# Cross-attention and routed experts: attention on pairs of head groups in five chunks of 128 keys, with the neighbouring block's raw-row transposes and router logits moved

## What is computed

```
x = x + xattn(layernorm(x), ctx)       # q, k, v; softmax(q k^T * scale) v; relu(out @ W1 + b1) @ W2 + b2
logits = layernorm(x) @ Wg.T ; top1 = argmax(logits)
x = x + expert[top1](layernorm(layernorm(x)))   # gelu((xhat * s_e + b_e) @ w1 + bb1) @ w2 + bb2
```

## Time and profile before

| | before |
|---|---|
| median of 3 runs | 1548.81 us (1548.56 to 1552.27) |
| the profiled execution | 1549.81 us, of which 1548.0 us are its span |
| PE busy | 1503.9 us (97%) |
| DVE busy | 1005.6 us (65%) |
| ACT busy | 711.5 us (46%) |
| chain that ended last | PE 78%, DVE 14% |

### The profile page before, as it was taken

How to read it: one execution, slowest core, us unless ns; L and a number is a source line. 1 busy time by engine, 2 the same in 40 slices (tenths; PEclk the granted TensorE clock), 3 DMA queues, 4 the chain that set the end, 5 groups by cost and what they waited for, 6 DMA issues and landing times.

```text
span 1548.0 us, 24311 instructions
## 1 busy us (share of the span) xinstructions
PE 1503.9 (97%) x7988; PEld 1257.0 (81%) x7988; DVE 1005.6 (65%) x2489; ACT 711.5 (46%) x2015; POOL 428.8 (28%) x312
## 2 busy tenths in 40 slices
PE   7689999999999999999999999999999999999998
PEld 4578888888888787878788888888887878778986
DVE  5735656575857576666757585757574756559666
ACT  3534535354536363545445353535363635424554
POOL 2512212222222222212122112222222222117776
PEclk9799999999999999999999999999999999999999
DMA  9310110213020202131211201030202011458883
GB/s 231 113 55 28 31 53 7 76 26 108 13 89 28 89 28 75 36 97 42 75 42 40 78 15 61 16 110 1 82 1 83 1 55 55 171 172 282 243 238 120
DMA packets 76951, 122.71 MB, mean 79 GB/s; under 512 B 27990, under 2 KB 36455, under 8 KB 75806
## 3 DMA queue, kind: packets, MB, share of 16 engines
q1 hardware_dynamic: 66030, 87.47, 19.6%
q0 software_dynamic: 10800, 33.70, 5.7%
HBM read 76.24 MB, written 46.72 MB: 79 GB/s over the span
## 4 chain that ended last, share of the span: by engine, by line
PE 78%; DVE 14%; ACT 4%; issue 2%; DMA 1%; POOL 1%; POOLq 0%; DVEq 0%; SPq 0%; ACTq 0%
PE bank L1034 23%; PE bank L1056 20%; PE bank L896 11%; PE bank L920 5%; PE bank L1014 5%; DVE actH L1003 4%; PE bank L1457 4%; PE bank L1501 3%; ACT actH L997 2%; PE bank L1125 2%; PE bank L1440 2%; PE bank L864 2%; DVE E L941 1%; DVE mx L929 1%; DVE sm L968 1%
## 5 line engine op out<-in xcount | busy, mean ns | idle before, releaser
L1056 PE MATMUL bank<-w,actH 128*128 128x512 f32 x1536 | 371.1, 392 | 0.0
L1034 PE MATMUL bank<-actA,w 128*128 128x512 f32 x1536 | 366.8, 394 | 0.0
L1034 PEld LDWEIGHTS bank<-actA,w 128*128 128x128 f32 x1536 | 286.0, 188 | 62.3
L1056 PEld LDWEIGHTS bank<-w,actH 128*128 128x128 f32 x1536 | 283.1, 188 | 54.9
L979 POOL TENSOR_TENSOR E<-E,rc 128x1232 f32<-128x1232 f32 x64 | 145.0, 2266 | 464.6 <-DVE rc L974 464.6
L1041 ACT ACTIVATE actH<-bank,b 128x512 fp32r<-128x512 f32 x128 | 88.2, 689 | 228.8 <-PE bank L1034 228.8
L1046 DVE TENSOR_TENSOR actH<-bank,actH 128x512 fp32r<-128x512 f32 x128 | 87.8, 686 | 159.6 <-ACT bank L1042 159.6
L896 PE MATMUL bank<-actA,wq 128*128 128x512 f32 x768 | 182.0, 390 | 0.0
L952 ACT ACTIVATE E<-bank,mx 128x77 f32<-128x77 f32 x512 | 157.8, 364 | 42.1 <-DVE mx L929 42.1
L896 PEld LDWEIGHTS bank<-actA,wq 128*128 128x128 f32 x768 | 144.1, 188 | 30.4 <-issue 0.5
L1199 POOL DMA_INDIRECT region<-rows,pos x64 | 62.3, 974 | 373.2 <-DVE pos L1193 334.0
(11 more groups left out here) (166 smaller groups left out, 1970.2 us busy)
## 6 DMA issues: line engine op xcount, KB each, us to landing
rowB<-region SPq DMA_DIRECT2D x71, 258.0 KB, 3.8
xn<-in_x SPq DMA_DIRECT2D x64, 256.0 KB, 2.8
rows<-in_x SPq DMA_DIRECT2D x64, 256.0 KB, 3.2
e_raw<-in_E SPq DMA_DIRECT2D x16, 256.0 KB, 2.8
region<-padrow SPq DMA_DIRECT2D x9, 258.0 KB, 3.9
w_raw<-in_W SPq DMA_DIRECT2D x1, 2048.0 KB, 11.8
w_raw<-in_W SPq DMA_DIRECT2D x2, 1024.0 KB, 8.7
e_parts<-e_high SPq DMA_DIRECT2D x8, 256.0 KB, 2.0
```

Of the source, the lines that this page charges most:

```text
L1034: mm = pe.matmul(p[:], w, a, start=k == 0 and j == 0, stop=k == KD - 1 and j == 2)
L1056: mm = pe.matmul(p[:], a, w, start=m == 0 and j == 0, stop=m == MF - 1 and j == 2)
```

## The change

The groups are taken in pairs: 616 keys of a pair are cut in five chunks, four of 128 and one of 104. Per pair one chunk (number 2, called C) holds keys of both groups, so its product goes to a bank of its own; chunks 0 and 1 (A) make the first group and 3 and 4 (B) the second. ACT copies the bank of C to a new tile `csb` (COPY), and two DVE additions (ADD) put its 32 rows for each group onto the banks of A and B. OUT takes the parts out as before. So a block has 10 PT steps in place of 12, and 30 AV matmuls in place of 36, and new are 2 copies and 4 additions on 32 partitions.

Of the four TT of the block before, two stay in the tail, with their take-out (TTOUT) at its end; two go behind H steps 0 and 1. H 0 and 1 are issued together, k by k. X2STAT starts after the tail. L moves from after H 0 to after H 2, LT to after H 3, RK to after H 5 (H 4 in the last block). E1_SUM moves from after H 1 to after H 2. The values are loaded in 24 transfers in place of 12. Banks are no longer given out in turn but as the bank that is left first by the order of the list.

```
-CH = [103, 103, 102]
+NP = KD // 2
+PH = 2 * HG
+CH = [128, 128, 128, 128, 104]
+CA, CC, CB = (0, 1), (2,), (3, 4)
...
         def attention_tail(b):
             for c in range(NC):
                 step("PT", b, 0, c)
             step("SUM", b, KD - 1)
+            for c in CA:
+                step("PT", b, 1, c)
+            step("AV", b, 0, "C")
+            step("COPY", b, 0)
+            step("AV", b, 0, "A")
+            step("AV", b, 0, "B")
             if b:
-                step("X2STAT", b - 1)
-            for g in range(KD):
-                if g + 1 < KD:
-                    for c in range(NC):
-                        step("PT", b, g + 1, c)
-                if b and g == KD - 2:
-                    for s in range(SUB):
-                        step("TT", b - 1, s)
-                step("AV", b, g)
+                step("TT", b - 1, 0)
+                step("TT", b - 1, 1)
+            step("AV", b, 1, "A")
+            step("ADD", b, 0, "A")
+            step("ADD", b, 0, "B")
+            step("OUT", b, 0, "A")
+            for c in CC + CB:
+                step("PT", b, 1, c)
+            step("AV", b, 1, "C")
+            step("OUT", b, 0, "B")
+            step("COPY", b, 1)
+            step("AV", b, 1, "B")
+            step("ADD", b, 1, "A")
+            step("ADD", b, 1, "B")
+            step("OUT", b, 1, "A")
+            step("OUT", b, 1, "B")
+            if b:
+                step("TTOUT", b - 1, 0)
+                step("TTOUT", b - 1, 1)
...
+            if b:
+                step("X2STAT", b - 1)
             for m in range(MF):
                 step("H", b, m)
-                if prep is not None and m == 1:
+                if prep is not None and m == 2:
                     step("E1_SUM", prep)
+                if b and m == 2:
+                    step("L", b - 1)
...
+                step("HLO", b, m)
+                if b and m == 1:
+                    for s in (2, 3):
+                        step("TT", b - 1, s)
+                        step("TTOUT", b - 1, s)
...
+        def dve_add(dve, b, pr, i):
+            p, r = of("AV", b, pr, i), slice(P - HD, P) if i == "A" else slice(0, HD)
+            if i == "A":
+                dve.wait_ge(S["act_c"], NP * b + pr + 1)
+            dve.wait_ge(S["pe_av"], av_count(b, pr, i))
+            dve.tensor_tensor(p[r, :], p[r, :], csb[r, :], ALU.add).then_inc(S["dve_c"], 1)
```

More of the change, by code:

```diff
@@ L360, in xattn_moe_kernel @@
                     step("E1_ACC", prep)
-                if prep is not None and m == 1:
+                if prep is not None and m == 2:
                     step("E1_CENTER", prep)
                     step("E1_STORE", prep)
-                if b and m == 2:
-                    step("LT", b - 1)
-                    step("HLO", b, m)
                 if b and m == 3:
                     step("DRAIN")
+                    step("OH", b - 1)
+                if b and m == (4 if last else 5):
                     for s in range(SUB):
@@ L372, in xattn_moe_kernel @@
                         step("XLOAD", b + 1)
-                if last and m == MF - KD:
+                if last and m == 5:
                     step("COUNT", 0)
                     step("TABLE1")
-                if m == 3 and not last:
+                    step("DRIP", 8)
+                if m == (3 if prep is None else 4) and not last:
                     step("XSTAT", b + 1)
@@ L476, in xattn_moe_kernel @@
         }
-        bank_of, before, users = {}, {}, [None] * 8
-        n = 0
-        for kind, *i in sched:
+        LEAVES = {"COPY": lambda b, p: ("AV", b, p, "C"), "OUT": lambda b, p, i: ("AV", b, p, i),
+                  "TTOUT": lambda b, s: ("TT", b, s), "HLO": lambda b, m: ("H", b, m), "Y": lambda b, s: ("YA", b, s),
+                  "E1_CENTER": lambda e: ("E1_SUM", e)}
+        left = {}
+        for place, (kind, *i) in enumerate(sched):
+            left[(kind, *i)] = place
+            if kind in LEAVES:
+                left[LEAVES[kind](*i)] = place
+        bank_of, before, users, busy = {}, {}, [None] * 8, list(range(-8, 0))
+        for place, (kind, *i) in enumerate(sched):
             if kind in freed:
                 key = (kind, *i)
[L483 to L486, removed]
+                n = busy.index(min(busy))
+                assert busy[n] < place
+                bank_of[key] = n
+                before[key] = users[n]
+                users[n] = freed[kind](*i)
+                busy[n] = left[key]
         def own_bank(eng, *key):
@@ new lines, in av_count, with pe_av @@
+        def av_count(b, pr, i):
+            return len(AV_ORDER) * b + AV_ORDER.index((pr, i)) + 1
+        def pe_av(pe, b, pr, i):
+            p = own_bank(pe, "AV", b, pr, i)
+            if (pr, i) == AV_ORDER[0]:
+                pe.wait_ge(ld_v, 16 * VLOADS * (b // BPB + 1))
+            mine = {"A": CA, "B": CB, "C": CC}[i]
+            for c in mine:
+                j = NC * pr + c
+                pe.wait_ge(S["dve_pt"], NC * NP * b + j + 1)
+                for t, (v, w) in enumerate(split3([vbd[0:CH[c], h, pr, c, :] for h in range(2)],
@@ L1013, in pe_av @@
                                                   [actH[0:CH[c], h, j % SLOTS, :] for h in range(2)])):
-                    mm = pe.matmul(p[:], v, w, start=c == 0 and i == 0, stop=c == NC - 1 and i == 2)
+                    mm = pe.matmul(p[:], v, w, start=c == mine[0] and t == 0, stop=c == mine[-1] and t == 2)
             mm.then_inc(S["pe_av"], 1)
-        def act_av(act, b, g):
-            act.wait_ge(S["pe_av"], KD * b + g + 1)
-            act.activation(actA[:, 0, g, :], of("AV", b, g)[:], ACT.Identity).then_inc(S["act_o"], 1)
@@ L1024, in dve_av @@
                               ).then_inc(S["dve_o"], 1)
         def pe_h(pe, b, m):
-            p = own_bank(pe, "H", b, m)
+            if m == 1:
+                return
+            mine = (0, 1) if m == 0 else (m,)
+            for m in mine:
+                own_bank(pe, "H", b, m)
             if b == 0:
```

155 lines of the change are left out of this document (89 added, 66 removed).

## The result

| | before | after |
|---|---|---|
| median of 4 runs | 1549.14 us | 1570.54 us (1569.91 to 1572.32) |
| ratio, 95% interval | | 1.0136 (1.0118 to 1.0153) |
| span of the profiled execution | 1548.0 us | 1568.2 us |
| PE busy | 1503.9 us (97%) | 1480.0 us (94%) |

A forecast was written before the change was run, and what follows sets the result against it. PE, busy 97% of the span, was taken to bound the kernel. Tail - 24, block 0 - 2 and waits for L + 42 made + 16 us on 1549.81, 1565.8, predicted as 1565; range 1547 to 1582 us.

The forecast's parts named there:

- The tail: First PT to first H: 13.6 us with waits of 0.5 and 0.7; 1.6 won per block, 24 in 15 blocks.
- Block 0: After its first low part, nine AV matmuls in place of 18: 2 us won, bounds 0.5 and 4.
- ADD: DVE additions in the tail: 0.61 us each, bounds 0.15 and twice 0.61, costing nothing.
- When L starts: In the up-projection L waits for DVE's last TT take-outs: 3.61 us in each of 8 blocks, 1.88 in 7; sum 42.1.
- e + 1.31: DVE starts taking out H 0's low part 1.31 us after e, the modelled end of H 0's last matmul.
- The clock: PE's clock behind the new waits for L: expected to stay up, granted clock 0.9 or more, nothing counted.
- my case: Main forecast for the whole kernel: 1565 us, itself 1553 to 1577, chance 0.55.
- a rival: PE's clock falls in the new waits in all eight blocks, 2 us each: 1581 us; chance 0.15.
- The sum: Whole kernel: - 24 - 2 + 42 = + 16 us against the profiled 1549.81.
- Transfers: 24 value transfers delay the row load some 8 us in blocks 3, 7, 11; nothing counted; rival 1571, chance 0.07.
- Banks: Banks given out differently: each former user taken out before PE comes to it, so nothing counted.

The follow-up runs named there:

- spread_only: Kernel before with only the spreading (two TT and X2STAT out of the tail; L, LT, RK, E1_SUM later), without pairs or interleaving; 1560.1 us.
- unmerged: Changed kernel with H 0 and H 1 issued one after the other; 1549.3 us.
- l_late2: Changed kernel with L behind H 3, LT and the one-hot behind H 4, and XSTAT behind H 4 in every block; 1538.1 us.
- filler: Changed kernel with 18 needless PE transposes ahead of the wait for L in the eight blocks with preparation; 1560.2 us.
- l2_split: l_late2 with the 24 value transfers cut in two, twelve behind the tail and twelve behind the next block's XLOAD; 1529.9 us.
- tt_in_tail: Changed kernel with all four TT in the tail and their take-outs at its end; 1566.2 us.

## Why the prediction was right, and where it was off

1565 was forecast and 1570.5 measured, inside the range; the direction and its reason held: L came late by the take-outs moved behind H 0 and H 1, and the loss was larger than the tail's gain. That it came so close is in part luck. The waits were 10 us shorter than forecast (32 against 42), and the clock, counted at nothing, cost 12. By its own steps:

- **The tail.** 13.6 us forecast, 13.66 measured in 15 blocks. The two waits in it were 0.33 and 0.63, not 0.53 and 0.7; the matmuls between them made up for it. What I booked wholly on the pairs is theirs only by half: spread_only, which has the old tail without two TT, needs 14.5 us for it. Taking eight transposes (0.79 us) and X2STAT out of the old tail saved 1.5 us, because waits went with them.
- **Block 0.** 2 us forecast; block 1's tail starts 2.2 us earlier (153.54 against 155.76). One profile of each can't say more than that: in the other runs with the same block 0 it starts anywhere from 151.6 to 153.4.
- **ADD.** 0.61 us and hidden. It takes 0.70, the same for 32 partitions as a take-out for 128, and in the change PE waits for none. It is hidden by the interleaving: in unmerged H 0 does wait, 0.4 us, for the take-outs behind the ADDs.
- **When L starts.** DVE took H 0 out at 337.76, which by my working is e + 1.31, so L could start 6.67 us later, at 344.43; it started at 344.18. The order of DVE and its prices were right to 0.25 us. The waits are shown as 0.49 and 2.26, 2.75 against my 3.61, and as 1.45 against 1.88. Part of that is the way of counting: the trace counts from the modelled end of the matmul before, I from where the next could have started. l_late2 shows what the wait of 1.45 truly cost, 1.57 us (82.1 to 80.53).
- **The clock.** This is the term that was mis-sized: my case had it at nothing, and a rival had it with a chance of 0.15 and 2 us. It fell in all eight blocks, at 1.4 to 1.7 us each, 12 us. Rival and case came true together: period + 2.8 to + 3.2 with preparation, where I had + 2.0, and + 0.1 where I had + 0.3. I had called the wait shorter than all that I saw followed by a low clock, and looked only at its longer piece.
- **The sum.** By the measured terms: tails 15 x 1.56 = - 23.4, block 0 - 2.2, waits 8 x 2.75 + 7 x 1.45 = + 32.2, clock + 12; that gives + 19, and the spans differ by 20.2. The agreement is closer than it should be. Where the last tail starts (1330.60 against 1307.53, 23.1 us later) the terms give 19, so 0.3 us a block is not in them, the way of counting above among it; and what follows that start is 2.9 us shorter (237.6 against 240.5 us). No run shows that to be the change's doing: in the filler the program there is the same, and that part took 240.7.
- **Transfers.** Rightly counted at nothing here. They take 0.80 us each, and the last rows' load starts 37.5 us behind the tail's start in place of 30.9 (355.29 and 350.58); yet blocks 3 and 7 were no longer than their neighbours. My reading, which no run tests by itself, is that with L's wait and the low clock ahead of them the statistics were asked for just as late; in the filler, where the clock stays up, block 3 is 1.4 us longer than its neighbours. Once the wait was gone they cost 8 us (l_late2 against l2_split).
- **Banks.** No wait on a bank turned up; the new rule was not tried apart.

## What to carry to other kernels

Before moving a step to a later place, write down what stands ahead of its last producer on the other engine's queue: here two take-outs moved from ahead of 2.70 us in which DVE stood idle to behind some 20 instructions, and 3% of the time lay in the order alone. A wait costs more than its length when the engine's clock falls behind it, so fill it with useful work or move its reader one step on; and look again at every queue after a wait is gone, because the next one (here 24 transfers ahead of a load) was hidden by it. When a change is split in parts, compare the parts place by place: two thirds of what spread_only lost stood behind the last tail, a place that the forecast had not counted. Interleaving two steps gives the engine that empties them both results late and at once; here it saved at most 0.4 us a block where nobody waited for that engine.

## What the runs showed of the hardware

- TensorE's clock fell to 1.2 GHz after idle times that were short: 0.49 and 2.26 us with the two matmuls of E1_SUM (0.67 us) between them, in eight of eight blocks; it did not after 1.46 us alone. In tt_in_tail it fell after 0.98 and 0.56 us in three blocks and not in the others with the same waits. What decides in the mixed blocks no run tells apart. The Trainium skill ("TensorE: Matmul & The Clock Gate", Part 1) says that the gate's rhythm runs on by itself and that the point at which the rate changes depends on where in it a kernel's first matmul lands; whether the same decides for waits inside a kernel no run here shows.
- Filling a wait with 18 needless transposes made the kernel 10.3 us faster.
- A DVE addition of 32 partitions by 512 elements from PSUM takes 0.70 us (64 of them, 687 to 716 ns), as a take-out of 128 partitions does.
